# Macaron block on one core: VectorE's order and the table of TensorE's side jobs rearranged

## The chip, the cores and the metric

The kernel runs on 1 core of one Trainium2 chip. The metric is device time in microseconds (us) of one execution. A difference is told against the kernel before.

## The reference

Per batch element (8 of them, 512 tokens, 256 features), in fp32: half a spectral feed-forward step, attention over the left 128 features (16 heads of 8), and half a feed-forward step again, each behind a layer norm and added to its input.

```python
def ffn(x):                       # _L0_ffn_ref
    x_freq = jnp.fft.fft(x, axis=-1)
    y_freq = jnp.einsum('bnd,do->bno', x_freq, w)      # w complex, 256x256
    return jnp.real(jnp.fft.ifft(y_freq, axis=-1)) + bias
x = L0_attn_x
x = x + 0.5 * ffn(_layernorm(x))
x = x + attn(_layernorm(x))       # q, k, v of left = x[..., :128]; softmax(q.k / 4); @ Wo.T + bo
x = x + 0.5 * ffn(_layernorm(x))
```

## The kernel before, in words

The FFT, the multiplication by w and the inverse FFT are folded once, in a prologue, into one real matrix `half_ffn`. After it one loop `for it in range(B)` treats attention of batch element `it` in 16 slots (`QUADS`). In each slot TensorE issues `score_quad` of the next slot (four matmuls of keys by queries into PSUM, L766), then the side jobs of this slot (L685 and a few others), then `value_quad` (four heads of probabilities by values, L779; a heading of a row may count them twice, since an fp32 matmul is two passes). ScalarE does the exponentials, two instructions a slot (L635). A ring of three score buffers and four probability buffers lies between the two.

The side jobs do all the rest of the block for other batch elements. The table `STEADY` names them by slot: a name, the distance d of the batch element from `it`, and a half of the one PSUM bank `misc`. `F1_i` is the first feed-forward step of token tile i of element it+2 (its two halves of the contraction are `F1_ia` and `F1_i`), `KT`, `QT` and `V` make k, q and v of it+2 or it+1 from `leftT`, `N` and `NT` make norms for a guard on the size of scores, `WO_i` is the output projection of it-1, `F2_i` the second feed-forward step of it-1. `BEGIN` and `END` are the tables of the first and last iteration. A job takes 8 or 16 rows of L685 matmuls; `a` halves, `V_i`, `QT_i`, `KT_i` and each half of an F step count 8, a `WO_i` 8 too. TensorE may start the jobs of slot s only when VectorE has taken everything of slot s-1 out of the bank (`pe.wait_ge(evacuated, count_of_slots_to(it, s - 1))` in `job`).

VectorE's program is in order too. At each slot it calls `run_jobs(it, s)`, which takes the jobs of the slot out of PSUM as soon as the slot's last job is done, and then does what stands by slot in its main loop: `take_values` (the attention output, after slots 7 and 15), `normalize`, `left_half` (the normed left half `lh` of it+2, four instructions at L900, which need the rstd that GpSimd computes), `turn_left` (its 32x32 block transpose, L908), `norm0_stats`. `turn_x2` (L914) turns the sum after attention for the second feed-forward step.

Transposes of whole matrices go over DRAM. SyncE (SP) issues these transfers from one queue in program order: `k_in`, `x2_through`, `xT_in_from`, `load_x`, `q_out`, `left_through` (which waits for `left_turned`), four of the eight `q_in` transfers (L382), `leftT_in` (L452), the other four `q_in`, then outputs. The queries `QS` of it+1 are needed by TensorE at `score_quad(it+1, 0)`, which it issues in slot 15 before the jobs; `leftT` of it+2 is needed by `KT_0` in slot 14.

GpSimd (POOL) computes rstd (`rstd_of`, L525 and L527), adds a row to x2 and x_out (`add_rows`, L530 and L540, two instructions each over 128x512), and squares k and q (L536).

In the first iteration `leftT` of element 2 comes over the same path. In the prologue TensorE runs `keep_awake` matmuls on a zero tile while nothing else is ready.

Of the kernel before, what the change touches and what calls it, by code (L numbers as in the profile page):

```python
# [28 lines left out]
B, S, E = 8, 512, 256  # L29
# [39 lines left out]
STEADY = {0: [("F1_0a", 2, LEFT)], 1: [("F1_0", 2, LEFT)], 2: [("WO_0", -1, LEFT), ("WO_1", -1, RIGHT)],  # L69
          3: [("WO_2", -1, LEFT), ("WO_3", -1, RIGHT)], 4: [("F1_1a", 2, LEFT), ("F1_1", 2, LEFT)],  # L70
          5: [("F1_2a", 2, LEFT), ("F1_2", 2, LEFT)], 6: [("F1_3a", 2, LEFT), ("F1_3", 2, LEFT)],
          7: [("QT_0", 1, LEFT)], 8: [("QT_1", 1, LEFT), ("V_0", 1, RIGHT)],
          9: [("V_1", 1, RIGHT), ("F2_0a", -1, LEFT)], 10: [("F2_0", -1, LEFT), ("N", 1, RIGHT)],
          11: [("NT", 1, RIGHT), ("F2_1a", -1, LEFT)], 12: [("F2_1", -1, LEFT)],
          13: [("F2_2a", -1, LEFT), ("F2_2", -1, LEFT)], 14: [("KT_0", 2, RIGHT), ("F2_3a", -1, LEFT)],
          15: [("F2_3", -1, LEFT), ("KT_1", 2, RIGHT)]}
# [101 lines left out]
def build_macaron(nc, x, x_t, wq_t, wk_t, wv_t, wo_rows, bo, w_re, w_im, bias, cos_var, sin_tab, ident_in,  # L178
# [14 lines left out]
    with ctx:  # L193
# [193 lines left out]
        def _(sp):  # L387
# [92 lines left out]
            for it in range(B):  # L480
# [30 lines left out]
        def _(pool):  # L511
# [31 lines left out]
            def end_of(b):  # L543
                rstd_of(2, b + 1)
# [99 lines left out]
        def _(pe):  # L644
# [203 lines left out]
            keep_awake(16)  # L848
# [3 lines left out]
            pe.wait_ge(late_loaded, 32)  # L852

# [26 lines left out]
        def _(dve):  # L880
# [16 lines left out]
            def left_half(b):  # L897
                dve.wait_ge(rstd_done[1], b + 1)
                for t in range(T):
                    last = nc.vector.tensor_scalar(lh[:, t, :], x1[b % 3][:, t, 0:HD], mv[1][:, t, 0:1],  # L900
                                                   rstd[1][0][:, t:t + 1], ALU.subtract, ALU.mult)
                last.then_inc(normed, 1)
# [189 lines left out]
            def run_jobs(it, s):  # L1092
# [3 lines left out]
                for name, b in evacuated_at(it, s):  # L1096
# [7 lines left out]
                    elif kind == "WO":  # L1104
                        if i == T - 1:
                            turn_x2(b, 0)
                            turn_x2(b, 1)
                        dve.wait_ge(evacuated, evac_count(name, b))
                        norm_stats(2, x2, i, i == T - 1)
                        if i == T - 1:  # L1110
                            norm_moments(2, b + 1)
# [45 lines left out]
            for it in range(B):  # L1157
                for s in range(QUADS):
# [9 lines left out]
                    if it == 0:  # L1168
# [5 lines left out]
                        if s == 9:  # L1174
                            left_half(2)
                            turn_left(2)
                    elif s == 8 and it + 2 < B:
                        left_half(it + 2)
                        turn_left(it + 2)
                    if s == 11 and it + 3 < B:  # L1180
                        norm0_stats(it + 3, range(0, 2))
                    if s == 12 and it + 3 < B:
                        norm0_stats(it + 3, range(2, T))
                        norm_moments(0, it + 4)
# [61 lines left out]
```

## Time and profile before

| | us |
|---|---|
| median of 3 runs (lowest to highest) | 340.14 (339.82 to 342.14) |
| the profiled execution, whole | 341.36 |
| its span (first to last instruction) | 339.5 |
| PE matmul busy | 307.1 (90%) |
| ACT busy | 250.2 (74%) |
| DVE busy | 189.9 (56%) |
| POOL busy | 112.3 (33%) |

The profile gives for each engine the time it was busy, and for each group of instructions what ended the idle time before it. PE is TensorE, DVE VectorE, ACT ScalarE, POOL GpSimd, SP SyncE. PEclk is the granted clock of TensorE as a share of full speed (1.00 is 2.4 GHz, 0.50 is 1.2 GHz). A row of the timeline has start, duration, engine, line, operation, tiles, count, and in brackets the idle time before it with what ended it.

### The profile page before, as it was taken

To read this page: it belongs to the slowest core of one execution; us is meant where nothing else is said; L and a number is where in the kernel's file an instruction comes from. 1 tells how busy PE (TensorE), PEld (TensorE's weight loads), DVE (VectorE), ACT (ScalarE), POOL (GpSimd) and SP (SyncE) were. 2 spreads that over 40 slices of the span, in tenths; PEclk is the share of its full clock that TensorE was granted. 3 is DMA by queue.
4 is the path that set the end of the run, shared out by engine and by line. 5 is a ranking of instruction groups with operands and counts; after the bars stand their busy time and mean duration, and the time that the engine had idled before them with its cause. 6 is when DMAs were issued, how large, how long until landed. Compare 5 with 4: busy or idle time off the path is not lost.

```text
span 339.5 us, 8953 instructions
## 1 busy us (share of the span) xinstructions
PE 307.1 (90%) x3469; PEld 117.1 (34%) x3473; DVE 189.9 (56%) x543; ACT 250.2 (74%) x266; POOL 112.3 (33%) x126
## 2 busy tenths in 40 slices
PE   8887699959999999899989999899989889998985
PEld 5642233213333333333333333333333323322333
DVE  1676555715685565755675577556563555353144
ACT  2100588958788788788779878888878998999931
POOL 5741451131451308050634136140810062007004
PEclk9999699989999999999999999999999999999999
DMA  7536829445677286538476487538354764303001
GB/s 213 209 125 200 175 94 180 163 126 128 121 251 215 99 139 237 185 97 191 117 268 173 136 146 245 178 136 130 124 167 117 184 159 141 112 2 124 33 34 62
DMA packets 30388, 50.40 MB, mean 148 GB/s; under 512 B 3840, under 2 KB 16512, under 8 KB 29440
## 3 DMA queue, kind: packets, MB, share of 16 engines
q1 hardware_dynamic: 28864, 48.13, 50.7%
q10 hardware_dynamic: 1472, 1.58, 2.0%
q8 instruction: 32, 0.52, 0.7%
q14 instruction: 20, 0.16, 0.1%
HBM read 31.87 MB, written 17.83 MB: 146 GB/s over the span
## 4 chain that ended last, share of the span: by engine, by line
PE 64%; DVE 18%; issue 7%; DMA 4%; ACT 3%; SPq 2%; POOL 1%; DVEq 0%; ACTq 0%; POOLq 0%
PE misc L685 24%; PE ot L779 23%; PE scores L766 11%; DVE x_blocks L914 3%; DVE lh L900 3%; ACT probs L635 3%; DVE stats L882 2%; SPq L382 2%; PE scores L652 2%; DVE VS L972 2%; PE scores L685 2%; DMA leftT<-left_scr 2%; DMA q_scr<-qp 1%; DVE x L935 1%; DMA QS<-q_scr 1%
## 5 line engine op out<-in xcount | busy, mean ns | idle before, releaser
L635 ACT ACTIVATE probs<-scores 128x1024 f32<-128x1024 f32 x256 | 245.0, 1027 | 55.4 <-PE scores L766 54.5
L779 PE MATMUL ot<-probs,VS 128*32 128x512 f32 x1024 | 137.6, 603 | 5.6 <-ACT probs L635 3.5
L766 PE MATMUL scores<-QS,KS 32*128 32x512 f32 x512 | 65.9, 502 | 3.5 <-DMA QS<-q_scr 1.8
L766 PEld LDWEIGHTS scores<-QS,KS 32*128 32x128 f32 x512 | 25.0, 183 | 112.2 <-ACT probs L635 99.5
L525 POOL TENSOR_SCALAR veps<-mv 128x4 f32<-128x4 f32 (+1 forms) x25 | 5.8, 230 | 159.7 <-DVE mv L889 159.7
L779 PEld LDWEIGHTS ot<-probs,VS 128*32 128x32 f32 x1024 | 32.0, 111 | 30.9 <-ACT probs L635 8.6
L685 PE MATMUL misc<-half_ffn,xT 128*32 128x256 f32 x448 | 34.8, 387 | 4.4 <-DVE VS L972 4.4
L959 DVE SCALAR_TENSOR_TENSOR x_out<-misc,rstd,x_out 128x256 f32<-128x256 f32 x28 | 13.6, 484 | 35.7 <-PE misc L685 29.6
L685 PE MATMUL misc<-half_ffn,xT_in 128*32 128x256 f32 x400 | 28.0, 386 | 5.7 <-DVE x L935 3.9
L527 POOL TENSOR_TENSOR rstd<-veps,power 128x4 f32<-128x4 f32 (+1 forms) x25 | 25.3, 1012 | 2.1
L882 DVE BATCH_NORM_STATS2 stats<-x 128x6 f32<-128x256 f32 x64 | 25.0, 413 | 0.1
L954 DVE TENSOR_TENSOR x<-misc,x 128x256 f32<-128x256 f32 x30 | 11.3, 420 | 21.8 <-PE misc L685 21.8
L935 DVE SCALAR_TENSOR_TENSOR x<-misc,rstd,x_in 128x256 f32<-128x256 f32 x24 | 11.5, 478 | 20.4 <-PE misc L685 20.4
L536 POOL TENSOR_TENSOR sq_k<-kp 128x512 bf16<-128x512 f32 x8 | 8.3, 1040 | 34.2 <-DVE kp L925 34.2
L530 POOL TENSOR_TENSOR x_out<-x,half_bias 128x512 f32<-128x512 f32 x9 | 11.6, 1284 | 17.8 <-DVE x L954 17.8
L925 DVE CAST kp<-misc 128x256 fp32r<-128x256 f32 x14 | 5.9, 422 | 19.6 <-PE misc L685 19.6
L685 PEld LDWEIGHTS misc<-half_ffn,xT 128*32 128x32 f32 x448 | 11.7, 108 | 14.6 <-DVE VS L972 5.9
L685 PE MATMUL misc<-wo_sb,otn 128*32 128x256 f32 x240 | 16.1, 385 | 0.6 <-DVE otn L1008 0.6
L685 PEld LDWEIGHTS misc<-half_ffn,xT_in 128*32 128x32 f32 x400 | 9.9, 109 | 17.1 <-DVE x L935 5.4
L994 DVE STREAM_TRANSPOSE ot_t<-ot 128x512 f32<-128x512 f32 x16 | 11.4, 712 | 7.0 <-PE ot L779 7.0
L659 PE MATMUL scores<-waking 128*128 128x512 bf16 x45 | 12.8, 430 | 2.5 <-issue 1.4
L914 DVE STREAM_TRANSPOSE x_blocks<-x 128x512 f32<-128x512 f32 x14 | 15.0, 1109 | 0.0
(109 smaller groups left out, 275.9 us busy)
## 6 DMA issues: line engine op xcount, KB each, us to landing
KS<-k_scr SPq DMA_DIRECT2D x56, 128.0 KB, 4.6
QS<-q_scr SPq DMA_DIRECT2D x56, 128.0 KB, 3.2
x_in<-x SPq DMA_DIRECT2D x8, 512.0 KB, 5.2
xT_in<-x_t SPq DMA_DIRECT2D x8, 512.0 KB, 5.8
k_scr<-kp SPq DMA_DIRECT2D x8, 512.0 KB, 2.7
q_scr<-qp SPq DMA_DIRECT2D x7, 512.0 KB, 3.5
x_scr<-x_blocks SPq DMA_DIRECT2D x7, 512.0 KB, 3.5
xT<-x_scr SPq DMA_DIRECT2D x7, 512.0 KB, 4.5
```

What stands on the lines that cost most here:

```text
L527: nc.gpsimd.tensor_tensor(to[:, tiles], veps[k][:, tiles], power[:, tiles], ALU.pow).then_inc(rstd_done[k], 1)
L530: nc.gpsimd.tensor_tensor(dst[:, tiles, :], src[:, tiles, :], row[:, :].unsqueeze(1).to_broadcast([P, tiles.stop - tiles.start, E]), ALU.a ...
L635: nc.scalar.activation(probs[u % PRING][:, :, :], scores[u % SRING][:, :, :], ACT.Exp, scale=SCORE_SCALE).then_inc(exp_done, 1)
L659: mm(bank, waking[:, 0:P], waking[:, :], start=True, stop=True)
L685: last = mm(dst[COL * j:COL * (j + 1), :], weights(j), rhs, start=c == 0, stop=c == len(terms) - 1)
L766: last = mm(scores[(u + j // 2) % SRING][:, j % 2, :], KS[b % 2][rows, slot, kt * P:(kt + 1) * P].bitcast(F32R), QS[b % 2][rows, slot, :]. ...
L779: last = mm(ot[COL * j:COL * (j + 1), :], VS[b % 2][:, kt, h, :], probs[(u + j // 2) % PRING][:, j % 2, :], start=s % 8 == 0, stop=s % 8 == 7)
L882: ins = nc.vector.bn_stats(stats[k][:, t, :], src[:, t, :])
L914: last = nc.vector.transpose(x2_blocks[:, :, 2 * i:2 * i + 2, :], x2[:, 2 * i:2 * i + 2, :].rearrange("p t (f k) -> p k t f", k=E // 32))
L935: return nc.vector.scalar_tensor_tensor(x1[b % 3][:, i, :], tile, rstd[0][b % 2][:, i:i + 1], biased[:, i, :], ALU.mult, ALU.add)
L959: nc.vector.scalar_tensor_tensor(x_out[:, i, :], tile, rstd[2][0][:, i:i + 1], x_out[:, i, :], ALU.mult, ALU.add).then_inc(evacuated, 1)
L994: nc.vector.transpose(ot_t[:, :, :].rearrange("p c r -> p (c r)"), ot[:, :]).then_inc(ot_taken, 1)
```

## The change

It changes nothing of what is computed. `STEADY` moves the two V jobs from slots 8 and 9 to slots 0 and 1 (of the same element it+1; `leftT_in` now waits for QT too, since QT comes last), gathers the F2 steps in slots 9 to 13, and leaves KT alone in 14 and 15. VectorE turns x2 in two pieces, in slots 2 and 3, and takes its statistics in slots 4 and 5; `left_half` is done in two steps in slots 8 and 9 with the turn in 9 (in iteration 0 all of it in slot 8, before it was slot 9); `normalize(it, 0)` goes from slot 8 to 14, `normalize(it, 1)` from slot 15 to slot 0 of the next iteration. GpSimd does both rstd first, then the x_out sum, the square of q, and the x2 sum. SyncE loads x of element 3 behind `q_out` in iteration 0. Two `keep_awake` calls get longer or are new.

```diff
-          7: [("QT_0", 1, LEFT)], 8: [("QT_1", 1, LEFT), ("V_0", 1, RIGHT)],
...
+STEADY = {0: [("V_0", 1, RIGHT), ("F1_0a", 2, LEFT)], 1: [("F1_0", 2, LEFT), ("V_1", 1, RIGHT)],
...
             def leftT_in(b):
-                sp.wait_ge(evacuated, last_count("V", b - 1))
+                for kind in ("V", "QT"):
+                    sp.wait_ge(evacuated, last_count(kind, b - 1))
...
-                if it + 3 < B:
+                if it >= 1 and it + 3 < B:
                     load_x(it + 3)
                 if it + 1 < B:
                     q_out(it + 1)
+                if it == 0:
+                    load_x(3)
...
             def end_of(b):
-                rstd_of(2, b + 1)
                 wait(pool, out_stored, 32 * b)
                 add_rows(x_out, x2, half_bias, x2b_done)
...
-                end_of(it - 1)
-                begin_x2(it)
+                rstd_of(2, it)
                 if it + 2 < B:
                     rstd_of(1, it + 3)
+                end_of(it - 1)
                 if it + 1 < B:
                     square(qp, sq_q, qp_step, it + 1)
+                begin_x2(it)
...
-            keep_awake(16)
+            keep_awake(20)
...
             pe.wait_ge(late_loaded, 32)
+            keep_awake(4, ot[:, :])
...
-                    elif kind == "WO":
-                        if i == T - 1:
-                            turn_x2(b, 0)
-                            turn_x2(b, 1)
...
+                    elif kind == "WO" and i % 2:
+                        turn_x2(b, i // 2)
...
-                    if s == 8:
+                    if s == 14:
                         normalize(it, 0)
-                    if s == 15 and it + 1 < B:
-                        normalize(it, 1)
...
+                    if s == 0 and it >= 1:
+                        normalize(it - 1, 1)
+                    if it >= 1:
+                        if s == 4:
+                            for t in range(2):
+                                norm_stats(2, x2, t, False)
+                        if s == 5:
...
+                    if it + 2 < B:
+                        if s == 8:
+                            left_half(it + 2, range(0, 2 if it else T))
+                        if s == 9 and it:
+                            left_half(it + 2, range(2, T))
+                        if s == (9 if it else 8):
+                            turn_left(it + 2)
```

VectorE's instructions in slots 8 to 11 of a steady iteration stood like this before, from the take of `QT_1` on (`x_2` is x1 of the element ahead, `lh` its normed left half, `norms` the result of job N):

```order
L925 CAST qp<-misc 128x256
L927 TENSOR_TENSOR qp<-misc,qp 128x256
L972 COPY VS<-misc 128x16x8 x2
L999 RECIPROCAL recip<-ot_t 128x32
L1002 TENSOR_TENSOR on<-ot_t,recip 128x16x16
L900 TENSOR_SCALAR lh<-x_2,mv,rstd_0 128x128 x4
L908 STREAM_TRANSPOSE left_blocks<-lh 128x512
L972 COPY VS<-misc 128x16x8 x2
L959 SCALAR_TENSOR_TENSOR x_out<-misc,rstd_0,x_out 128x256
L977 TENSOR_REDUCE norms<-misc 128x1
```

The same stretch of VectorE now:

```order
L929 CAST qp<-misc 128x256
L931 TENSOR_TENSOR qp<-misc,qp 128x256
L903 TENSOR_SCALAR lh<-x_2,mv,rstd_0 128x128 x2
L963 SCALAR_TENSOR_TENSOR x_out<-misc,rstd_0,x_out 128x256
L903 TENSOR_SCALAR lh<-x_2,mv,rstd_0 128x128 x2
L912 STREAM_TRANSPOSE left_blocks<-lh 128x512
L981 TENSOR_REDUCE norms<-misc 128x1
L963 SCALAR_TENSOR_TENSOR x_out<-misc,rstd_0,x_out 128x256
```

The two V copies and the normalization are gone from here, the four `lh` instructions stand two before and two behind the first take of F2, and the take of N stands right behind the turn.

GpSimd's instructions of one steady iteration, from the rstd of x2 to the square of q, before:

```order
L525 TENSOR_SCALAR veps<-mv 128x4
L527 TENSOR_TENSOR rstd_0<-veps,power 128x4
L540 TENSOR_TENSOR x_out<-x,half_bias 128x512
L530 TENSOR_TENSOR x_out<-x,half_bias 128x512
L540 TENSOR_TENSOR x<-x_2,bo_sb 128x512
L530 TENSOR_TENSOR x<-x_2,bo_sb 128x512
L525 TENSOR_SCALAR veps<-mv 128x4
L527 TENSOR_TENSOR rstd_0<-veps,power 128x4
L536 TENSOR_TENSOR sq_q<-qp 128x512
```

And now:

```order
L527 TENSOR_SCALAR veps<-mv 128x4
L529 TENSOR_TENSOR rstd_0<-veps,power 128x4
L527 TENSOR_SCALAR veps<-mv 128x4
L529 TENSOR_TENSOR rstd_0<-veps,power 128x4
L542 TENSOR_TENSOR x_out<-x,half_bias 128x512
L532 TENSOR_TENSOR x_out<-x,half_bias 128x512
L538 TENSOR_TENSOR sq_q<-qp 128x512
L542 TENSOR_TENSOR x<-x_2,bo_sb 128x512
L532 TENSOR_TENSOR x<-x_2,bo_sb 128x512
```

The second rstd (of x1, which `left_half` waits for) moved ahead of the four sums, and the square of q stands between the sum into x_out and the sum into x2.

## Rows read from the trace of the kernel before

**Rows 1.** Busy time of five stretches (79.20 to 263.88), iterations 1 to 5, with sum and mean.
```profile
sum 184.68, PE 174.32 PEld 64.46 DVE 115.19 ACT 154.26 POOL 63.07; mean PE 34.86 PEld 12.89 DVE 23.04 ACT 30.85 POOL 12.61
```
**Rows 2.** Timeline of PE, iteration 2: value quads, stalls, and the next element's first scores.
```profile
130.54 1.04 PE L779 MATMUL ot<-probs,VS 128*32 128x512 f32 x8
...
132.41 1.04 PE L779 MATMUL ot<-probs,VS 128*32 128x512 f32 x8
...
134.71 1.04 PE L779 MATMUL ot<-probs,VS 128*32 128x512 f32 x8
...
139.54 0.64 PE L685 MATMUL misc<-half_ffn,xT 128*32 128x256 f32 x8 [0.87 <-DVE VS L972]
...
149.56 0.50 PE L766 MATMUL scores<-QS,KS 32*128 32x512 f32 x4
...
164.15 1.07 PE L685 MATMUL misc<-half_ffn,xT_in 128*32 128x256 f32 x16 [0.78 <-DVE x L935]
```
**Rows 3.** Timeline of DVE, iterations 2 and 3.
```profile
130.79 0.48 DVE L935 SCALAR_TENSOR_TENSOR x<-misc,rstd,x_in 128x256 f32<-128x256 f32 x1 [1.48 <-PE misc L685]
...
131.97 0.38 DVE L889 BATCH_NORM_AGGREGATE mv<-stats 128x2 f32<-128x6 f32 x4
...
136.88 1.11 DVE L900 TENSOR_SCALAR lh<-x,mv,rstd 128x128 f32<-128x128 f32 x4
138.03 1.09 DVE L908 STREAM_TRANSPOSE left_blocks<-lh 128x512 f32<-128x512 f32 x1
...
160.86 2.14 DVE L914 STREAM_TRANSPOSE x_blocks<-x 128x512 f32<-128x512 f32 x2
```
**Rows 4.** Timeline of POOL, iteration 3: rstd and the sum into x_out.
```profile
163.81 0.23 POOL L525 TENSOR_SCALAR veps<-mv 128x4 f32<-128x4 f32 x1 [10.74 <-DVE mv L889]
...
165.13 1.28 POOL L540 TENSOR_TENSOR x_out<-x,half_bias 128x512 f32<-128x512 f32 x1
```
**Rows 5.** Timeline of all engines, ahead of iteration 0: `lh` beside POOL's sums.
```profile
35.04 1.27 POOL L540 TENSOR_TENSOR x<-x,bo_sb 128x512 f32<-128x512 f32 x1
35.10 3.02 DVE L900 TENSOR_SCALAR lh<-x,mv,rstd 128x128 f32<-128x128 f32 x4 [1.48 <-POOL rstd L527]
...
36.27 1.26 POOL L530 TENSOR_TENSOR x<-x,bo_sb 128x512 f32<-128x512 f32 x1
```
**Rows 6.** Timeline of POOL, iteration 6: the square of q.
```profile
280.82 1.05 POOL L536 TENSOR_TENSOR sq_q<-qp 128x512 bf16<-128x512 f32 x1
```
**Rows 7.** Timeline of SP, iteration 2, and L382's times to landing in iteration 4.
```profile
139.14 0.33 SPq L446 DMA_DIRECT2D left_scr<-left_blocks  x1
...
142.59 2.41 SPq L382 DMA_DIRECT2D QS<-q_scr  x4
...
DMA to landing us min/median/max: 2.5/3.0/4.4
```
**Rows 8.** Timeline of iteration 0, PE alone: the wait for leftT and the iteration's end.
```profile
73.27 0.64 PE L685 MATMUL misc<-leftT,wk_sb 128*32 128x256 f32 x8 [3.45 <-DMA leftT<-left_scr]
...
79.09 1.07 PE L779 MATMUL ot<-probs,VS 128*32 128x512 f32 x8
```
**Rows 9.** Timeline of SP, iteration 0.
```profile
65.06 0.33 SPq L446 DMA_DIRECT2D left_scr<-left_blocks  x1
```
**Rows 10.** Timeline of PE, start of iteration 0.
```profile
35.29 0.73 PE L766 MATMUL scores<-QS,KS 32*128 32x512 f32 x4 [1.61 <-DMA QS<-q_scr]
37.23 0.80 PE L766 MATMUL scores<-QS,KS 32*128 32x512 f32 x4 [1.21 <-ACT probs L635]
38.27 1.08 PE L722 MATMUL misc<-ident,lh 128*128 128x128 f32 x4 [0.24 <-DVE lh L900]
...
44.47 0.64 PE L685 MATMUL misc<-leftT,wk_sb 128*32 128x256 f32 x8
```
**Rows 11.** By stretch: length, PE, PEld, DVE, ACT, POOL, PEclk, DMA share, GB/s.
```profile
38.00:40.00 2.00, 1.76 (x11) 0.91 (x12) 0.73 (x2) 1.93 (x3) 0.00 (x0) 0.50 1.07 227
...
74.00:76.00 2.00, 2.00 (x16) 0.37 (x12) 0.81 (x2) 0.00 (x0) 0.00 (x0) 0.53 0.00 0
```

More of the change, by code:

```diff
@@ L62 @@
 LEFT, RIGHT = 0, 1
-STEADY = {0: [("F1_0a", 2, LEFT)], 1: [("F1_0", 2, LEFT)], 2: [("WO_0", -1, LEFT), ("WO_1", -1, RIGHT)],
-          3: [("WO_2", -1, LEFT), ("WO_3", -1, RIGHT)], 4: [("F1_1a", 2, LEFT), ("F1_1", 2, LEFT)],
-          5: [("F1_2a", 2, LEFT), ("F1_2", 2, LEFT)], 6: [("F1_3a", 2, LEFT), ("F1_3", 2, LEFT)],
-          7: [("QT_0", 1, LEFT)], 8: [("QT_1", 1, LEFT), ("V_0", 1, RIGHT)],
[L73 to L76, printed above, removed]
+STEADY = {0: [("V_0", 1, RIGHT), ("F1_0a", 2, LEFT)], 1: [("F1_0", 2, LEFT), ("V_1", 1, RIGHT)],
+          2: [("WO_0", -1, LEFT), ("WO_1", -1, RIGHT)], 3: [("WO_2", -1, LEFT), ("WO_3", -1, RIGHT)],
+          4: [("F1_1a", 2, LEFT), ("F1_1", 2, LEFT)], 5: [("F1_2a", 2, LEFT), ("F1_2", 2, LEFT)],
+          6: [("F1_3a", 2, LEFT), ("F1_3", 2, LEFT)], 7: [("QT_0", 1, LEFT)], 8: [("QT_1", 1, LEFT)],
+          9: [("F2_0a", -1, LEFT), ("F2_0", -1, LEFT)], 10: [("N", 1, RIGHT), ("F2_1a", -1, LEFT)],
+          11: [("F2_1", -1, LEFT), ("NT", 1, RIGHT)], 12: [("F2_2a", -1, LEFT), ("F2_2", -1, LEFT)],
+          13: [("F2_3a", -1, LEFT), ("F2_3", -1, LEFT)], 14: [("KT_0", 2, RIGHT)], 15: [("KT_1", 2, RIGHT)]}
 BEGIN = {0: [("LT", 1, LEFT)], 1: [("KT_0", 1, LEFT)], 2: [("KT_1", 1, LEFT)],
@@ L895, in norm0_stats, with left_half @@
                     norm_stats(0, x_in[b % 2], t, t == T - 1)
-            def left_half(b):
+            def left_half(b, tiles=range(T)):
                 dve.wait_ge(rstd_done[1], b + 1)
-                for t in range(T):
+                for t in tiles:
                     last = nc.vector.tensor_scalar(lh[:, t, :], x1[b % 3][:, t, 0:HD], mv[1][:, t, 0:1],
                                                    rstd[1][0][:, t:t + 1], ALU.subtract, ALU.mult)
-                last.then_inc(normed, 1)
+                if tiles[-1] == T - 1:
+                    last.then_inc(normed, 1)
             def turn_left(b):
@@ L1163, in _ @@
                         take_values(it, 1)
-                    if s == 8:
+                    if s == 14:
                         normalize(it, 0)
-                    if s == 15 and it + 1 < B:
-                        normalize(it, 1)
-                    if it == 0:
+                    if s == 0 and it >= 1:
[5 more added lines that the diff above has]
+                        if s == 5:
+                            for t in range(2, T):
+                                norm_stats(2, x2, t, t == T - 1)
+                            norm_moments(2, it)
+                    else:
                         if s == 0:
@@ L1173, in _ @@
                             norm_moments(0, 3)
[L1174 to L1184, printed above, removed]
+                    if it + 2 < B:
[5 more added lines that the diff above has]
+                            turn_left(it + 2)
+                    if it + 3 < B:
+                        if s == 11:
+                            norm0_stats(it + 3, range(0, 2))
+                        if s == 13:
+                            norm0_stats(it + 3, range(2, T))
+                            norm_moments(0, it + 4)
                     if s == GUARD_SLOT and it + 1 < B:
```

4 lines of the change are left out of this document (removed).

## The prediction, made before the changed kernel ran

> **What bounds the kernel now.** I read the busy times by iteration first. Iterations 1 to 5 are the five full uses of `STEADY`; together they last 184.68 us, 36.94 each, with TensorE matmuls busy 34.86 and ScalarE 30.85 of that [rows 1]. So TensorE's program order sets the pace, ScalarE has some 6 us of room, and VectorE (23.04) matters only where it holds the bank `misc`.
>
> Second, TensorE's timeline, for the price of a slot. The value quad of slot 7 follows that of slot 6 after 1.87 us with 8 rows of jobs between, that of slot 8 follows after 2.30 with 24 matmul rows in two jobs [rows 2] (16 rows in the program's count, the V job being half as wide). So a slot with one unit of jobs takes 1.86, with two units 2.30. In both tables STEADY has 26 units: ten slots with two, six with one. N and NT add 0.28 (an estimate from what is left of the spacing of their slots). Without any wait an iteration would be 10 x 2.30 + 6 x 1.86 + 0.28 = 34.4 us. The difference to 36.94 is 2.5 us a turn of waits for VectorE. Two of them are the largest: 0.87 before the jobs of slot 10, behind V_1, and 0.78 before F1_2 in slot 5 [rows 2]. VectorE's rows say why: before V_1's take it does four `lh` (1.11) and the turn (1.09), and before F1_1's take both turns of x2 (2.14) [rows 3]. The rest are some tenths in slots 9, 12 and 0.
>
> **The change, part by part.** I follow one steady iteration from o, the moment VectorE starts to take F1_3 in slot 6; in iteration 2 that is 130.79 [rows 3].
>
> *x2 in two pieces, statistics in 4 and 5, V in 0 and 1, both normalizations moved.* A two-unit slot leaves VectorE 2.30 us. Slots 2 and 3 now hold two takes of 0.42 and a turn of 1.07, slot 5 at most a take of 0.48, three statistics at about 0.38 and moments of 0.38: all under 2.30. So the waits of slots 5, 9, 10 and 0 go: -2.5 us a turn. The work moved is the same work; its cover is TensorE's 1.3 us of value and score quads after each job.
>
> *The left half in slots 8 and 9 beside a reordered GpSimd.* This is the part I find dear. The moments of x1 are done at o + 1.56 (131.97 + 0.38) [rows 3]. GpSimd's rstd takes 1.32 from its start to the next instruction [rows 4]; started at o + 1.65, the two sums into x_out run from o + 2.97 to 5.50 (1.24 apart), the square of q (1.05 [rows 6], and 1.03 to the next) until 6.5, and the sums into x2, which stood ahead of this before, from 6.45 to 8.97. Now VectorE: QT_1 is alone in slot 8, so its take starts at o + 3.73 and ends at 4.6, and `lh` follows. `lh` beside GpSimd's sums is seen once before: four instructions took 3.02 us where they take 1.11 alone; the sums stood at 35.04 and 36.27, and `lh` from 35.10 to 38.12 [rows 5, 3], so each sum let one `lh` through at its end (two blocked ones 1.2 us each, two free ones 0.28). With this, lh 0 ends at o + 5.55, lh 1 behind the square at 6.57, the take of F2_0 (due at 6.02) runs until 7.0, lh 2 ends behind the first x2 sum at 7.8, lh 3 behind the second at 9.05, and the turn (1.09) ends at 10.15. Before it ended at 139.12 = o + 8.33. If the square blocks nothing, lh 1 ends 0.7 earlier, and nothing later moves.
>
> The Trainium skill (page "SBUF — State Buffer", section "SBUF: two separate sides") says that VectorE and GpSimd share one port pair as an exclusive lock, held for a whole instruction, which fp32 operations of VectorE with one SBUF source in a two-port mode, or with two SBUF inputs, ask for. The row agrees. By it the iteration is what this sum gives; if `lh` ran freely it would be the second rival below.
>
> *What queues behind.* On VectorE: the take of N in slot 10. It starts at 10.17 instead of 8.0 and ends at 10.58. TensorE would start slot 11's jobs at o + 9.15 (slot 9's jobs from 4.88, then 1.00 + 1.29 + 0.68 + 1.29) and starts them at 10.63: **a new wait of 1.48**.
> On SP: `left_through` waits for the turn, and all `q_in` stand behind it. From its issue (139.14) to the last QS issue (142.59 + 1.81) are 5.26 us, and the slowest landing of a group was 4.4 [rows 7] (3.7 to 4.5 over the iterations, a reading of the same view; I take 4.2). So the last query lands at 10.17 + 5.26 + 4.2 = o + 19.6. Slot 15's score quad needs it. Before it was issued at 149.56 = o + 18.77 [rows 2], with the waits of slots 9, 10 and 12 inside. Now, with slots 11 to 14 behind the new wait (10.63, then 0.77 + 2.29 + 2.29 + 1.86, and 0.86 of value quad), it is due at 18.7: **a second new wait of 0.9** (0.4 to 1.2).
>
> One iteration: 34.4 + 1.48 + 0.9 = 36.8. Iteration 5 has one unit less (its slot 0 successor has V alone): 36.4. Five: 4 x 36.8 + 36.4 = 183.6, against 184.7: **-1.1 us**. Iteration 6, with few jobs, and 7 stay: there no left half is made, and ScalarE paces the empty slots.
>
> *Iteration 0.* KT_0 waits 3.45 us for leftT [rows 8], because `left_through` is issued at 65.06 [rows 9] behind a turn that VectorE does after slot 9. With the turn after slot 8 the left half starts when the rstd of x1 is there, about 59.9, with GpSimd idle, and the turn ends at 62.15: 2.9 us earlier. TensorE's wait shrinks to 0 to 0.5. Then the first scores of element 1 wait for the last queries, at 62.2 + 5.3 + 3.7 = 71.2 to 71.9, not 75.2; in addition the clock stood at 0.5 from 74.2 to 77.6 [rows 11], after that idle time, and one pair of slots took 1.1 us more. The value quad that starts at 79.09 [rows 8] would start at 74.7: **-4.4 us** (3.3 to 5).
>
> *keep_awake.* TensorE idled 1.61 and 1.21 us around its first scores [rows 10], and the clock was 0.50 from 36.6 to 43.4 [rows 11]. Four more matmuls ahead and four behind fill 1.7 of that; they end before the rows land and before the first exponentials, so they cost nothing. At full clock, from LT at 38.27: 0.45, 0.86, 0.43, 0.57, 0.86, 0.43 bring the job that started at 44.47 [rows 10] to 41.87: **-2.6 us**; if the clock falls all the same, 0.
>
> Sum: -1.1 - 4.4 - 2.6 = -8.1. Against the profiled execution's 341.36 that is 333.3; the median of the runs is 340.14, so 332.
>
> **The rivals.**
> A, the forecast: 332, its own range 328.5 to 335.
> B, the left half runs mostly free (GpSimd's order falls otherwise, or the squares and sums let more than one `lh` pass). The turn ends at o + 8.3; N is in time; the queries land at 17.8 against a need of 17.2: 34.4 + 0.6 = 35.0 a turn, so 9 us less over five: 324 to 326. For it: 7 of the 8 groups of four `lh` before were free. Against: they were free because GpSimd idled at 136.88, and now four long instructions of it lie there.
> C, the clock falls at the start of iteration 0 all the same: 334.6. The window of 38 to 40 had TensorE busy for 1.76 of 2 us at 0.50 [rows 11], so it depends on what came before it.
> D, the change doesn't bring its gain in iteration 0 either (leftT lands slowly, 5.2 instead of 3.6, and the queries behind it), or the steady waits come 0.8 larger each: 337 to 341.
> E, slower: TensorE now idles 1.48 in slot 11 and 0.9 in slot 15 of each turn. Where it idled 3.45 us the clock fell to half for 3.4 us [rows 8, 11], which cost 1.6 us (1.36 + 0.73 + 1.01 + 1.19 instead of 0.86 + 0.43 + 0.57 + 0.86, a reading of the chain). If these waits did the same twice a turn, 5 x 3.2 = 16 us: 348. It decides from one fall a turn, 8 us. Against: waits of 0.8 to 1.2 a turn stood here before at a clock of 1.00 throughout, and 1.48 is far from 3.45.
>
> **How the numbers follow.** A 0.50, B 0.20, C 0.14, D 0.11, E 0.05. The predicted time is A's, 332. The range takes in A, C, most of B and the near end of D: 325 to 337.5. A change of 1%, 3.4 us, is about what a measurement of this kernel can tell from none. Faster than 336.7: A, B, C, 0.83. Within 1%: most of D, 0.12. Slower than 343.5: 0.05.
>
> **What would show it.** Steady iterations of 36.8 with no wait in slot 5 and none behind V, but a wait of TensorE for `norms` before the jobs of slot 11, about 1.5, and one for QS in slot 15, near 0.9; `lh` at a mean above 0.8 us each in iterations 1 to 5; the turn's end 10.15 behind F1_3's take. leftT waited for under 0.6 us in iteration 0; the clock at 1.00 from 36 to 78. I am wrong if `lh` stays at 0.28 each (then B), if the clock row shows 0.50 at 38 (C) or in steady iterations (E), or if slots 0 to 3 show waits for VectorE that I costed at nothing: there its load is within 0.3 us of the slot in slots 2, 3 and 5.

## The result and the profile after

The changed kernel takes 336.27 us (median of 20 runs), the kernel before 340.13 (20 runs): a ratio of 0.9881 with a 95% interval of 0.9858 to 0.9905, so 4.0 us or 1.2% faster. The ratio leaves out the slow runs (three of the 20 after, up to 351.6, and two of the 20 before), which the medians include. The forecast was 8.1 us less, 332; the sign holds, the size is half, and 336.3 lies above rival A's own range (328.5 to 335) and just below rival D's (337 to 341). The profiled execution took 335.66 (its span 333.9), against 341.36 (339.5) for the profiled execution before: this pair differs by 5.7, since the one profiled before is 1.2 above its median and the one after is 0.6 below.

The page of the changed kernel, its part 1, and the clock row of its part 2:

```profile
PE 302.7 (91%) x3477; PEld 115.7 (35%) x3481; DVE 208.2 (62%) x543; ACT 250.0 (75%) x266; POOL 112.6 (34%) x126
PEclk9999999999999999999999999999999999999999
```

VectorE has 18.3 us more busy time than before (189.9) with the same work on it. Most of it is one group. The page after, its part on groups (count, busy, mean ns of one):

```profile
L903 DVE TENSOR_SCALAR lh<-x,mv,rstd 128x128 f32<-128x128 f32 x32 | 26.2, 868 | 1.8 <-POOL rstd L529 1.8
```

Before, the same group was 10.8 us at 400 ns. (One `lh` alone has a duration of 0.34 us and the next one starts 0.28 behind it, so four take 1.11.) The clock is at its upper level throughout, 2.4 GHz.

The five steady iterations (71.98 to 256.65) have not become shorter. Busy time by stretch after, the first of them and the sum (columns as in [rows 11], the sum line as in [rows 1]):

```profile
71.98:108.93 36.95, 34.69 (x427) 12.88 (x423) 27.64 (x68) 30.85 (x33) 13.41 (x14) 1.00 0.61 166
...
sum 184.67, PE 173.10 PEld 64.25 DVE 134.66 ACT 153.82 POOL 63.23; mean PE 34.62 PEld 12.85 DVE 26.93 ACT 30.76 POOL 12.65
```

184.67 against 184.68. What TensorE waits for has changed, though. Two of its waits before (total, times, longest):

```profile
PE misc L685 <- DVE VS L972: 4.6, 6, 0.9
PE misc L685 <- DVE x L935: 3.9, 5, 0.8
```

Neither is left. Its waits after:

```profile
PE misc L687 <- DVE norms L981: 6.0, 5, 1.3
PE scores L768 <- DMA QS<-q_scr: 3.7, 4, 1.6
PE misc L687 <- DMA leftT<-left_scr: 2.5, 3, 1.5
PE misc L687 <- DMA xT<-x_scr: 2.0, 2, 1.6
```

TensorE's timeline after, some rows: the start, the end of iteration 0, the two waits of iteration 2, one of iteration 5 and one of iteration 6.

```profile
41.66 0.64 PE L687 MATMUL misc<-leftT,wk_sb 128*32 128x256 f32 x8
...
71.98 1.04 PE L781 MATMUL ot<-probs,VS 128*32 128x512 f32 x8
...
133.49 0.64 PE L687 MATMUL misc<-half_ffn,xT 128*32 128x256 f32 x8 [1.30 <-DVE norms L981]
...
143.26 0.50 PE L768 MATMUL scores<-QS,KS 32*128 32x512 f32 x4 [1.62 <-DMA QS<-q_scr]
...
252.40 0.64 PE L687 MATMUL misc<-leftT,wk_sb 128*32 128x256 f32 x8 [1.54 <-DMA leftT<-left_scr]
...
275.37 1.07 PE L687 MATMUL misc<-half_ffn,xT 128*32 128x256 f32 x16 [1.61 <-DMA xT<-x_scr]
```

The value quad that stood at 79.09 [rows 8] stands at 71.98, and the job of 44.47 [rows 10] at 41.66. So in the pair of traces everything is won by the end of iteration 0 (-7.1), nothing in iterations 1 to 5, and iteration 6 gives 1.6 back (from value quad to value quad 33.7 us, 32.1 before).

The mechanism inside a steady iteration is the one forecast, row by row. VectorE's timeline after, iteration 2; the take of F1_3 at 122.95 is o:

```profile
122.95 0.48 DVE L939 SCALAR_TENSOR_TENSOR x<-misc,rstd,x_in 128x256 f32<-128x256 f32 x1 [0.41 <-PE misc L687]
...
127.48 2.03 DVE L903 TENSOR_SCALAR lh<-x,mv,rstd 128x128 f32<-128x128 f32 x2
129.43 0.47 DVE L963 SCALAR_TENSOR_TENSOR x_out<-misc,rstd,x_out 128x256 f32<-128x256 f32 x1
129.83 2.17 DVE L903 TENSOR_SCALAR lh<-x,mv,rstd 128x128 f32<-128x128 f32 x2
132.03 1.10 DVE L912 STREAM_TRANSPOSE left_blocks<-lh 128x512 f32<-128x512 f32 x1
133.04 0.39 DVE L981 TENSOR_REDUCE norms<-misc 128x1 f32<-128x256 f32 x1
```

The same stretch of GpSimd after:

```profile
125.90 1.29 POOL L542 TENSOR_TENSOR x_out<-x,half_bias 128x512 f32<-128x512 f32 x1
127.14 1.30 POOL L532 TENSOR_TENSOR x_out<-x,half_bias 128x512 f32<-128x512 f32 x1
128.38 1.05 POOL L538 TENSOR_TENSOR sq_q<-qp 128x512 bf16<-128x512 f32 x1
129.37 1.30 POOL L542 TENSOR_TENSOR x<-x,bo_sb 128x512 f32<-128x512 f32 x1
130.60 1.30 POOL L532 TENSOR_TENSOR x<-x,bo_sb 128x512 f32<-128x512 f32 x1
```

GpSimd runs without a gap from 125.90 to 131.9. The first two `lh` end at 129.5 (behind the second x_out sum and the square) and the last two at 132.0 (behind both x2 sums), about 1.0 to 1.1 us each where they take 0.28 alone. The turn ends at 133.13 = o + 10.18. The take of F2_0 at 129.43, which reads PSUM, lies beside the first x2 sum and keeps its length (0.47); the turn and the take of N come when GpSimd has finished.

### The profile page after: what moved, and what is told of

It reads as the page before. It is cut to its first block, busy times and chain, and to the rows that moved or that the text cites. A ratio compares the mean times of both kernels' runs of the same rounds, so it can differ in the third digit from the quotient of the medians.

```text
span 333.9 us, 8968 instructions
## 1 busy us (share of the span) xinstructions
PE 302.7 (91%) x3477; PEld 115.7 (35%) x3481; DVE 208.2 (62%) x543; ACT 250.0 (75%) x266; POOL 112.6 (34%) x126
## 4 chain that ended last, share of the span: by engine, by line
PE 51%; DVE 16%; DMA 15%; SPq 7%; issue 6%; ACT 3%; POOL 1%; DVEq 0%; ACTq 0%; POOLq 0%
PE misc L687 20%; PE ot L781 18%; PE scores L768 9%; SPq L381 6%; DVE lh L903 6%; DMA QS<-q_scr 4%; DMA xT<-x_scr 3%; DMA leftT<-left_scr 3%; DMA x_scr<-x_blocks 3%; ACT probs L637 2%; DMA x_in<-x 2%; DVE left_blocks L912 2%; PE scores L687 2%; DVE stats L885 1%; POOL rstd L529 1%
## 5 line engine op out<-in xcount | busy, mean ns | idle before, releaser
L781 PE MATMUL ot<-probs,VS 128*32 128x512 f32 x1024 | 135.6, 595 | 5.0 <-ACT probs L637 3.7
L768 PE MATMUL scores<-QS,KS 32*128 32x512 f32 x512 | 65.0, 495 | 4.6 <-DMA QS<-q_scr 3.7
L781 PEld LDWEIGHTS ot<-probs,VS 128*32 128x32 f32 x1024 | 31.1, 109 | 28.4 <-ACT probs L637 9.4
L687 PE MATMUL misc<-half_ffn,xT 128*32 128x256 f32 x448 | 31.4, 385 | 8.0 <-DVE norms L981 6.0
L903 DVE TENSOR_SCALAR lh<-x,mv,rstd 128x128 f32<-128x128 f32 x32 | 26.2, 868 | 1.8 <-POOL rstd L529 1.8
L885 DVE BATCH_NORM_STATS2 stats<-x 128x6 f32<-128x256 f32 x64 | 23.4, 412 | 0.1
L918 DVE STREAM_TRANSPOSE x_blocks<-x 128x512 f32<-128x512 f32 x14 | 16.2, 1157 | 0.5
```

What stands on the lines that cost most here:

```text
L687: last = mm(dst[COL * j:COL * (j + 1), :], weights(j), rhs, start=c == 0, stop=c == len(terms) - 1)
L768: last = mm(scores[(u + j // 2) % SRING][:, j % 2, :], KS[b % 2][rows, slot, kt * P:(kt + 1) * P].bitcast(F32R), QS[b % 2][rows, slot, :]. ...
L781: last = mm(ot[COL * j:COL * (j + 1), :], VS[b % 2][:, kt, h, :], probs[(u + j // 2) % PRING][:, j % 2, :], start=s % 8 == 0, stop=s % 8 == 7)
L885: ins = nc.vector.bn_stats(stats[k][:, t, :], src[:, t, :])
L918: last = nc.vector.transpose(x2_blocks[:, :, 2 * i:2 * i + 2, :], x2[:, 2 * i:2 * i + 2, :].rearrange("p t (f k) -> p k t f", k=E // 32))
```

## The experiments

Each was compared with the kernel before on the same chip. "After" below is the changed kernel; times are medians, with the ratio to before and its 95% interval. Since before's median on those occasions lay between 340.4 and 342.1, a difference is worked out as the ratio times 340.1 us; for after, that is -4.0. "Iteration n lasts" means from the first scores of element n to those of the next.

**Is it the collision of `lh` with GpSimd? e1_x2sum_waits: after, with GpSimd's x2 sums held until all `lh` are done.**

```diff
                 if it + 1 < B:
                     square(qp, sq_q, qp_step, it + 1)
+                if it + 2 < B:
+                    pool.wait_ge(normed, it + 3)
                 begin_x2(it)
```

> The changed kernel, with GpSimd's sum into x2 held back until the left half of slots 8 and 9 is done. Theory (GpSimd's running instruction blocks each left-half instruction until it ends): the first two stay slow, near 1 us each, since the sum into x_out and the square of q still run there; the last two fall from 1.1 to 0.28 us each, the turn ends some 1.6 us earlier, TensorE's wait for the norms before slot 11 falls from 1.3 us to under 0.2, and the span falls by 6 to 9 us. Rival (the left half is slow for a reason of its own, such as the transfers or its place on VectorE): all four stay near 1 us and the time stays within 1 us of the changed kernel.

Measured 327.99, ratio 0.9617 (0.9569 to 0.9664): 13.0 us under before and 9.0 under after, as expected, from one wait on an engine that is busy for a third of the time. VectorE's timeline in this kernel, iteration 2:

```profile
126.42 2.04 DVE L905 TENSOR_SCALAR lh<-x,mv,rstd 128x128 f32<-128x128 f32 x2
...
128.78 0.59 DVE L905 TENSOR_SCALAR lh<-x,mv,rstd 128x128 f32<-128x128 f32 x2
129.40 1.17 DVE L914 STREAM_TRANSPOSE left_blocks<-lh 128x512 f32<-128x512 f32 x1
```

and GpSimd's:

```profile
127.32 1.05 POOL L538 TENSOR_TENSOR sq_q<-qp 128x512 bf16<-128x512 f32 x1
129.45 1.28 POOL L542 TENSOR_TENSOR x<-x,bo_sb 128x512 f32<-128x512 f32 x1 [1.07 <-DVE lh L905]
```

The first two `lh` still take 1.0 each, beside the x_out sum and the square; the last two, with GpSimd idle from 128.4, take 0.29 each. Same instructions, same kernel, 2 us apart: what differs is GpSimd. Iterations 1 to 5 last 36.1, 35.4, 35.4, 35.6 and 36.3 us (after: 36.9, 37.5, 36.7, 36.4, 37.4). No wait for `norms` is left; leftT is waited for 0.5 to 1.6 us in slot 14.

**Does the order of GpSimd's work do it as well? e2_pool_order: after, with before's order of the first steps (rstd of x2, x_out sums, rstd of x1), then the square, then the wait of e1.**

```diff
                 rstd_of(2, it)
+                end_of(it - 1)
                 if it + 2 < B:
                     rstd_of(1, it + 3)
-                end_of(it - 1)
                 if it + 1 < B:
                     square(qp, sq_q, qp_step, it + 1)
+                if it + 2 < B:
+                    pool.wait_ge(normed, it + 3)
                 begin_x2(it)
```

> The changed kernel, with GpSimd's order rstd of x2, sum into x_out, rstd of x1, square of q, and the sum into x2 only after the left half. Theory: at most one of four left-half instructions is blocked (by the square), the mean falls from 1.0 to under 0.5 us, the turn ends near 8.3 us behind the take of F1_3 instead of 10.2, no wait for the norms, and what is left is the wait for the queries in slot 15 of 0.3 to 0.9 us; 327 to 330 us. Rival (the queries' own chain, from their store to the last landing, sets the iteration): the left half is fast but the time stays above 333 us.

Measured 329.43, ratio 0.966 (0.9606 to 0.9715), 7.5 us under after. The mean of `lh` is 510 ns (after 868). Steady iterations last 35.4 to 35.7, but iteration 6 lasts 34.0, with 1.87 us of waiting for xT. It is no faster than e1: 1.4 us longer by the medians, with intervals that overlap. So the order of the first steps matters little beside the wait on the x2 sums.

**All four `lh` in one go: e8_left_at_once.** After, all of `lh` in slot 8, the turn in 9; GpSimd waits for them ahead of the square and the x2 sums.

```diff
                     square(qp, sq_q, qp_step, it + 1)
...
+                if it + 2 < B:
+                    pool.wait_ge(normed, it + 3)
...
-                            left_half(it + 2, range(0, 2 if it else T))
-                        if s == 9 and it:
-                            left_half(it + 2, range(2, T))
+                            left_half(it + 2)
```

(The wait stands ahead of `square`.)

> The changed kernel with all four left-half instructions in slot 8 (the turn stays in 9) and GpSimd waiting for them ahead of the square of q and of the sum into x2. Theory (the port): one or two of the four are blocked by the sum into x_out, the other ones take 0.28 us, the turn ends 0.7 us earlier than with the sum into x2 alone held back, waits for leftT and QS shrink by as much: 324.5 to 327.5 us. Rival (with the turn this early the store of q and the transfers themselves set slots 14 and 15): within 1 us of 328.

Measured 328.27, ratio 0.9615 (0.9561 to 0.967), as e1 and as the rival had it (the interval, 325.2 to 328.9 us, does not shut the theory's range out); iterations 1 to 5 last 35.1 to 35.6, and iteration 6 has a wait of 0.90 for xT. Two rows of VectorE's timeline in it, slots 8 and 14 of iteration 3:

```profile
162.52 1.81 DVE L905 TENSOR_SCALAR lh<-x,mv,rstd 128x128 f32<-128x128 f32 x4
...
176.34 1.26 DVE L1008 TENSOR_TENSOR on<-ot_t,recip 128x256 f32<-128x256 f32 x1
```

Four `lh` in 1.81: one blocked, three free. The second row is the next collision of the same kind: `normalize`, now in slot 14, meets GpSimd's sums of `next_x`, and `on` takes 1.26 where its shortest is 0.42. Both sides of it were moved by the change, which also takes the second half of `norm0_stats` in slot 13 where it was slot 12, and `next_x` waits for these statistics.

**Iteration 6: e9_after_f2_later.** After, with a table of its own for the last iteration but one, where F2 stands one slot later (10 to 14).

```diff
+LATE = dict(STEADY)
+LATE.update({9: [], 10: [("N", 1, RIGHT), ("F2_0a", -1, LEFT)], 11: [("F2_0", -1, LEFT), ("NT", 1, RIGHT)],
+             12: [("F2_1a", -1, LEFT), ("F2_1", -1, LEFT)], 13: [("F2_2a", -1, LEFT), ("F2_2", -1, LEFT)],
+             14: [("F2_3a", -1, LEFT), ("F2_3", -1, LEFT)]})
...
-    table = BEGIN if it == 0 else END if it == B - 1 else STEADY
+    table = BEGIN if it == 0 else END if it == B - 1 else LATE if it == B - 2 else STEADY
```

> The changed kernel with the F2 jobs one slot later in iteration 6 alone (slots 10 to 14). Theory (the transposed x2 lands too late for slot 9 in this iteration, whose slots are short): no wait of TensorE for xT in iteration 6 (1.61 us before), period of iteration 6 near 32.3 us instead of 33.7, and 1 to 1.6 us off the time of the changed kernel. Rival (the iteration is set by the queries of element 7): the xT wait goes and a wait in slot 15 of about the same size takes its place, no difference.

Measured 335.15, ratio 0.9807 (0.9758 to 0.9856), 1.1 us under after's median and 2.5 by the ratios. Iteration 6 lasts 32.05 (after 33.74) with no wait for xT; the steady ones stay at 36.8 to 37.6. So some 1.1 to 2.5 us of after's time is xT arriving late in iteration 6; its trace showed 1.6.

**Both together: e10_left_at_once_f2_later,** the edits of e8 and e9.

> The kernel of e8_left_at_once with the F2 jobs of iteration 6 one slot later as well. Theory: a wait for xT in iteration 6, where it stands, goes; 0.3 to 1.6 us less than e8_left_at_once. Rival: no difference, since that wait comes in only some executions and an early landing leaves nothing to gain.

Measured 326.51, ratio 0.9568 (0.9516 to 0.962), 1.8 us under e8, which ran beside it.

**And `on` out of GpSimd's way: e12_no_port_in_14,** e10 with the sums of `next_x` held until the attention output of slot 14 is normalized.

```diff
-            def next_x(b):
+            def next_x(b, behind=0):
...
+                wait(pool, ot_step, behind)
...
-                    next_x(it + 3)
+                    next_x(it + 3, 4 * it + 2)
```

> The kernel of e10_left_at_once_f2_later with GpSimd's sum into x_in held back until the normalization of slot 14 is done. Theory (the normalization, a product of two SBUF tiles, is blocked there as the left half was): it falls from 1.26 to 0.43 us, TensorE's wait of 0.42 us for the take of KT_1 goes in the iterations that have it, and the time falls by 1 to 2 us, to 324.5 to 325.5 us. Rival (the transfers for slots 14 and 15 take the place of that wait): within 0.7 us of 326.5.

Measured 325.24, ratio 0.9569 (0.9512 to 0.9626), the shortest median of the study, 14.7 us or 4.3% under before. The group of `on` in e10 and in e12, each from its own kernel's groups:

```profile
L1012 DVE TENSOR_TENSOR on<-ot_t,recip 128x256 f32<-128x256 f32 x16 | 11.1, 692 | 0.5
```

```profile
L1013 DVE TENSOR_TENSOR on<-ot_t,recip 128x256 f32<-128x256 f32 x16 | 7.1, 446 | 0.5
```

Iterations 2 to 5 last 34.9 each, near the 34.4 that the prediction took for an iteration with no wait at all. TensorE's wait behind the take of KT_1 is gone: the slot that takes 2.8 us in iterations 3 to 5 of e10 takes 2.3 in e12. But iteration 1 lasts 36.2 (e10: 35.4), with 1.20 us of waiting for queries at its end instead of 0.50. Against e10 the median is 1.3 lower, but the two did not run side by side and their ratios are alike, so what this last edit is worth in time is not settled. That `on` runs shorter is.

**The clock at the start: e3_before_awake (before, with the two `keep_awake` edits alone) and e4_after_no_awake (after, without them).**

```diff
-            keep_awake(16)
+            keep_awake(20)
...
             pe.wait_ge(late_loaded, 32)
+            keep_awake(4, ot[:, :])
```

> The kernel before with only the two longer keep_awake calls of the change. Theory: the clock stays at 1.00 at the start of iteration 0 and the time falls by 2 to 2.6 us against the kernel before. Rival (in most executions of the kernel before the clock does not fall there, or ScalarE sets the pace of these slots): under 0.7 us.

> The changed kernel with keep_awake as before (16 matmuls, none behind the first scores). Theory: the clock falls to 0.5 near 36 us again and the time rises by 2 to 2.6 us over the changed kernel. Rival: no difference above 0.7 us, since the clock or ScalarE's pace takes it up.

e4 took 338.78, ratio 0.9944 (0.9896 to 0.9992): 2.1 above after by the ratios, 2.5 by the medians, with the clock at 0.57 from 38 to 42 in its trace. So in after the edit is worth something, and by these values nearly what it was costed at (2.6), though the intervals of the two ratios just overlap. Not all of it need be won at the start. e4's trace is 3.0 us longer than after's; 1.9 of that is there by the first scores of element 1, and 1.8 comes in iteration 6, where the clock fell a second time, behind a wait for xT. TensorE's row and the stretches of 2 us around it (columns as in [rows 11]; in after the wait in this place is 1.61 and the clock stays at 1.00):

```profile
276.84 1.62 PE L687 MATMUL misc<-half_ffn,xT 128*32 128x256 f32 x16 [1.77 <-DMA xT<-x_scr]
```

```profile
276.00:278.00 2.00, 1.16 (x16) 0.88 (x20) 0.00 (x0) 1.08 (x2) 1.80 (x2) 0.80 0.65 240
278.00:280.00 2.00, 2.00 (x15) 0.27 (x5) 0.48 (x1) 0.00 (x0) 0.00 (x0) 0.50 0.24 66
```

But e3 took 340.54, ratio 1.0 (0.9972 to 1.0029, 10 runs): in before the edit is worth nothing that shows, at most 1.0 us, and the rival held. Its trace has the clock at 1.00 from 34 to 44 and the first scores of element 1 at 72.94 (75.19 before), so 2.3 us are won there; in iteration 6 it waits 0.99 us for xT, and the profiled run (338.8) is the fastest of the ten. The mean granted clock did rise: six of the ten ran at 0.994 or 0.995 (median 339.8) and four at 0.989 or 0.990 (341.5), where before has 0.990 (339.7) and 0.985 (341.6). So the low stretch at the start is gone and the time is not. A second trace of this kernel:

> The kernel of e3_before_awake once more, for a second trace, since its profiled execution was the fastest of its ten. Theory (what keep_awake gains at the start is given back by waits for the queries in slot 15 and for xT in iteration 6, which come and go with the transfers): the first scores of element 1 come near 73 us again, and if the time is above 340 us, some period of iterations 1 to 6 is 0.5 to 1.2 us longer by such a wait. Rival (the clock falls elsewhere in a slow execution): the granted clock is below 0.994 and the periods of iterations 1 to 6 are as in the first trace.

This execution took 342.73, with 1.27 for xT in iteration 6 (TensorE's timeline of e3_again):

```profile
283.04 0.64 PE L685 MATMUL misc<-half_ffn,xT 128*32 128x256 f32 x8 [1.27 <-DMA xT<-x_scr]
```

Before element 1, where TensorE stands idle for leftT as it does in before, the clock was at 0.50 from 70 to 76, longer than in the first trace (0.56 and 0.59 from 70 to 74), and the first scores of element 1 came at 74.5, 0.9 of it because those of element 0 were later too; slot 15 waited 0.84, 0.18 and 0.36 us in iterations 1 to 3. So both explanations have a part in it, the clock and the transfers, and their shares stay open.

**Iteration 0: e5_before_left_early.** Before, with the left half, its turn and the load of x as in after in iteration 0 alone.

```diff
-                if it + 3 < B:
+                if it >= 1 and it + 3 < B:
                     load_x(it + 3)
...
+                if it == 0:
+                    load_x(3)
...
-                        if s == 9:
+                        if s == 8:
```

(The last edit is the condition of iteration 0's left half.)

> The kernel before with only the part of the change that touches iteration 0: the left half of element 2 made after slot 8 instead of 9, and x of element 3 loaded behind the store of q. Theory (iteration 0 is held by the chain from the left half over DRAM to k): TensorE's wait for leftT in iteration 0 falls from 3.45 us to under 0.8, the clock does not fall near 74 us, first scores of element 1 come 3 to 4 us earlier, and the time falls by 3 to 4.4 us. Rival (the queries of element 1, which are loaded in the same stretch, hold it anyway): the wait for leftT goes and one for QS of 2 us or more comes, gain under 1.5 us.

Measured 338.12, ratio 0.9867 (0.9804 to 0.9931), 4.5 us under before. The wait for leftT is gone; in its trace the first scores of element 1 wait 0.57 us for the queries. The first scores of element 1 come at 73.04, 2.2 us earlier than in before where 3 to 4 were expected; those of element 0 were 1.0 later in this trace. The clock still fell at the start, at 38 to 44, as in before, and did not at 74.

**All but the steady part: e11_before_all_but_steady,** before with the edits of e3 and e5.

> The kernel before with the parts of the change that lie outside its steady iterations: keep_awake, the left half of element 2 after slot 8, x of element 3 behind the store of q. Theory (the changed kernel gains all its time ahead of iteration 1, and its steady iterations and iteration 6 give some of it back): 6 to 7 us under the kernel before, so 2 to 3 us under the changed kernel. Rival (keep_awake is worth nothing here, as e3_before_awake says): 4 us under the kernel before, the same as the changed kernel, and the steady part then neither gains nor loses.

Measured 336.93, ratio 0.9899 (0.9854 to 0.9943): 3.4 us under before, not 7, so nearer to the rival. In its trace the first scores of element 1 come at 69.28, 5.9 us earlier than in before. Then it gives back: slot 15 takes 2.59, 3.01 and 3.24 us in iterations 1 to 3 where it takes 2.30 without a wait (before: 2.77, 2.29 and 2.29), and iteration 6 waits 0.83 us for xT. The second trace:

> The kernel of e11_before_all_but_steady once more, for a second trace. Theory: waits for the queries in slot 15 add 1 to 2.5 us over iterations 1 to 5 again, but not in the same iterations, as they depend on how the transfers fall. Rival (they are fixed by the kernel's order): the same iterations show the same waits within 0.2 us.

One execution, 337.16. Slot 15 took 2.29, 2.30 and 3.48 this time, so it waited in iteration 3 alone, and iteration 6 for 0.93. The waits for queries change from run to run, in part (iteration 3 has one in both); that for xT is in both.

## Why the prediction was right and wrong

**Right: the mechanism of the steady iteration.** The turn ended at o + 10.18 for 10.15; the wait in front of slot 11's jobs was there in all five iterations, up to 1.30 us, for 1.48; slots 0 to 9 have no wait for VectorE, as costed; one late query wait of 1.62 stands in iteration 2. `lh` at 1.0 to 1.1 us each in these iterations (868 ns over all 32) for "above 0.8". The square of q does block `lh`, which the prediction left open. The rule of the Trainium skill (page "SBUF — State Buffer", section "SBUF: two separate sides"), that VectorE and GpSimd take one port pair in turns, each for a whole instruction, is borne out here: e1, e8 and e12 held GpSimd back and each got the short durations back (0.29 for `lh`, 0.42 for `on`). Rival B, `lh` mostly free, was refuted for this kernel, and the steady iteration that it priced, 35.0, is near that of e1, e8 and e12: 35.4 to 36.3, 35.1 to 35.6, and 34.9 in four of five.

**Right: iteration 0, the start and the clock, in the trace.** The value quad is 7.1 us earlier for 7.0 (2.6 + 4.4); 2.8 of it at the job of 44.47. Rivals C and E fell: PEclk is at 1.00 throughout, beside waits of 1.3 and 1.6 us. (What E describes did come once elsewhere, in iteration 6 of e4's trace. Its cost of one fall, 1.6 us, is 1.7 by its own four terms.)

**Wrong, first term: "a second new wait of 0.9".** The steady sum -1.1 measured 0.0. The spacing of score quads shows the two waits apart. Behind slot 11's jobs it is 3.4 in four of five iterations and 3.0 in the fifth where e12, without the wait, has 2.06: 6.4 us over five iterations, for 7.4. From slot 14's jobs to the next first scores it is 2.97, 3.55, 2.78, 2.47 and 3.47 where 1.86 is unhindered: 5.9 us, 1.2 a turn, for 4.5. The working took leftT for hidden, and the issue of the queries for as short as before. SyncE's timeline after, iteration 2:

```profile
133.15 0.33 SPq L445 DMA_DIRECT2D left_scr<-left_blocks  x1
133.53 3.05 SPq L381 DMA_DIRECT2D QS<-q_scr  x4
136.69 0.52 SPq L452 DMA_DIRECT2D leftT<-left_scr  x1
137.25 2.49 SPq L381 DMA_DIRECT2D QS<-q_scr  x4
```

From the store of the left half to the end of the last issue it is 6.6 us, and 6.4 to 7.0 over the five iterations. The row of before that the prediction read (139.14 to 142.59 + 2.41) gives 5.9; its 5.26 counts to the start of the last issue, which is 6.0 here. So the issue is 0.7 longer, in this iteration at the first four queries (3.05 for about 2.4), in others at the last four; the last landing, 4.1, is as costed, and this 0.7 is the difference between the wait of 1.62 and the forecast 0.9. leftT stands between the two groups of queries, and from its issue to its landing it takes 4.5 us (median of 6, 3.2 to 5.4), 3.6 before (3.3 to 5.2). So KT_0 in slot 14 waits for it in three iterations (1.54 us in iteration 5) and takes part of what the queries would have been waited for. Of the 1.1 missing, 1.4 is more there, 1.0 is less behind slot 11's jobs, 0.4 is a wait for xT in slot 9 of iteration 4 (0.34, which nothing in the sum had), and 0.3 is the five iterations without waits, 34.5 each instead of 34.4.

**Wrong, second term: "Iteration 6, with few jobs, and 7 stay".** It was a 0 and measured +1.6. The prediction looked at the units of jobs there but not at x2's way over DRAM. F2 stands from slot 9 on in both kernels, but without the V jobs slots 8 and 9 are shorter and TensorE needs xT 0.7 us sooner. SyncE issues the store of x2 and then the load. SyncE's timeline before, iteration 6:

```profile
273.55 0.34 SPq L434 DMA_DIRECT2D x_scr<-x_blocks  x1
276.37 0.65 SPq L440 DMA_DIRECT2D xT<-x_scr  x1
```

and after:

```profile
258.57 3.60 SPq L374 DMA_DIRECT2D KS<-k_scr  x8
...
265.37 0.34 SPq L433 DMA_DIRECT2D x_scr<-x_blocks  x1
270.60 0.65 SPq L439 DMA_DIRECT2D xT<-x_scr  x1
```

The load, which waits for the store, is issued 5.2 us behind it instead of 2.8, and slots 4 to 6 of this iteration have no jobs, so TensorE is early. e9 took the wait away, and time with it. A second thing was not to be seen in one trace: that before has no such wait in iteration 6 of its profiled execution was no slack. Five more traces have before's iteration 6 in every line. The four of e3 and e11 show 0.83 to 1.27 us of this wait, with the load 4.5 to 4.6 behind the store; that of e5 has 3.1 there and no such wait, but 1.13 for the queries at the end. In all five the iteration lasts 33.9 to 34.3, where it is 32.85 in before's trace and 33.74 in after's. So much of the 1.6 is a low value of the one trace that the sum was set against, and less of it is the change's.

**Wrong, third term: -2.6 and -4.4 as time of the whole kernel.** They are there in the traces at the end of iteration 0: the value quad of 79.09 stands at 71.98 in after and at 72.11 in e11. But e11 is 3.4 us under before (1.9 to 5.0), where 7.0 was summed. e5 alone gives 4.5 (2.3 to 6.7), as costed; e3 alone gives 0 for the 2.6. The sum of the two measured is within e11's interval, so they may add. What is missing in before is the part of `keep_awake`. What comes early in the traces meets waits for queries and for xT later on; the term failed by being summed against a trace whose later iterations had been taken as fixed. The prediction had priced rival D, "doesn't bring its gain in iteration 0 either", at 0.11 and for another reason, slow landings of leftT and of the queries in iteration 0. Its other half, steady waits that "come 0.8 larger each", measured 0.3 larger for the one and smaller for the other.

**The account.** The sum had -8.1 against the profiled execution. In the pair of traces it is -7.1 + 0.0 + 1.6 and -0.1 behind it = -5.6, the difference of the spans, so 2.5 of the 4.1 missing are in rows: 1.1 in iterations 1 to 5, 1.6 in iteration 6, and -0.1 each ahead of them and behind. The other 1.6 is that this pair lies further apart than the two kernels do. The prediction took differences within before's trace off before's median, and that trace was of the longer kind, with more time at the lower clock for the change to win back. In the ratios it is -4.0, of which e11 has -3.4. The rest, the rearrangement of VectorE's order and of the job table itself, is 0.6 us in its favour by the ratios 0.9881 and 0.9899, whose intervals overlap, so it may be nothing. It had removed 2.5 us of waits a turn and made 2.5 us of others.

**What stays open:** why leftT takes longer to land in after, why the store of x2 in iteration 6 takes 2.8 us until its load can go in one trace and up to 5.2 in another, and why the queries take longer to issue (no run changed the load on the queues alone); and whether `keep_awake` is really worth more in after (2.1, with intervals that just overlap) than in before (0, at most 1.0), where one trace shows 2.3 us won by the first scores of element 1 and the traces show only part of what takes them back.

## What to carry to other kernels

Before an operation of VectorE on SBUF alone is moved, look at what GpSimd runs beside its new place, and price each blocked one at what is left of GpSimd's instruction and its own time behind it, a whole instruction for each in a row of them; if they meet, let the engine with room wait (here one wait, -9.0 us, more than the whole change brought). When a compute wait on the path is removed, the transfers that came due behind it are the next bound: price them with their longest landing and their longest issue time (here the landing was priced so and held, the issue was not). A transfer that nobody waits for in one trace isn't thereby early, and a gain at the start is only time when nothing after it waits for something that did not move.

## What the runs showed that was not expected

- Blocked `lh` and GpSimd alternate, one `lh` at the end of each GpSimd instruction, and the wait stands in the row as a longer duration, never as idle time: VectorE's busy time rose by 18.3 us with no work added, of which `lh` has 15.4. A busy share can hold blocked time.
- The same holds for `on` (two SBUF inputs, one of them broadcast): 0.42 us alone, 0.77 to 1.47 beside a sum of GpSimd in after. It depends on how much of the sum is left: in all four cases `on` ends 0.28 to 0.29 us behind the sum's end. And it goes both ways. The sum that follows takes 1.46 to 1.48 where it takes 1.28 in e12, with `on` out of its way. VectorE and GpSimd after, iteration 1:

```profile
105.25 1.31 DVE L1006 TENSOR_TENSOR on<-ot_t,recip 128x256 f32<-128x256 f32 x1
```

```profile
105.01 1.26 POOL L542 TENSOR_TENSOR x_in<-x_in,half_bias 128x512 f32<-128x512 f32 x1
106.24 1.46 POOL L532 TENSOR_TENSOR x_in<-x_in,half_bias 128x512 f32<-128x512 f32 x1
```

- Not lengthened beside GpSimd's sums: statistics (two in 0.75 us at 324.95 in after), the turn of the left half (1.08 to 1.09 in e12, beside the square and an x2 sum), and takes that read PSUM (0.47 at 129.43 in after).
- The kernel before runs at a mean granted clock of 0.985 or of 0.990, about as often: its executions beside e1 to e12 have a median of 341.6 us at the one (16 of them) and 339.7 at the other (17). The profiled one, with 0.985, was of the longer kind, and so the pair of traces differed by 5.7 where the ratio says 4.0. After ran at 1.00 in most executions.
